# First feed-forward block of a Macaron layer: x kept whole in SBUF, ACT takes half of the norm and the weight copies, column sums in parts, semaphores cleared by ranges

## The reference

```python
x = x + 0.5 * ffn(layernorm(x), router_w, w1, w2)
x = x + mamba(layernorm(x), ...)
x = x + 0.5 * ffn(layernorm(x), router_w, w1, w2)

def ffn(x, router_w, w1, w2):        # 8 experts, hidden 512, top 2
    logits = x @ router_w.T
    top_vals, top_idx = top_k(logits, 2); top_w = softmax(top_vals)
    y[e] = relu(x @ w1[e])**2 @ w2[e]
    return sum over the two chosen experts of top_w * y[expert]
```

## Time and profile before

| what | us |
|---|---|
| three runs | 1326.93, 1328.05, 1328.78 |
| profiled execution | 1326.81, its span 1325.1 |
| first FFN, front | 4 to 71.4 |
| first FFN, sort and pieces | 71.4 to 85.1 and to 109.4 |
| first FFN, experts, to the last scatter | 117.7 to 373 |
| Mamba | 381.4 to 951 |
| second FFN, sort and pieces | 957 to 972.8 and to 997.1 |
| second FFN, experts and end | 1005 to 1258 and to 1325.1 |
| busy over the span | TensorE 1055.2, VectorE 822.2, ACT 607.5, POOL 686.4 |

### The profile page before, as it was taken

How to read it: one execution, slowest core, us unless ns; L and a number is a source line. 1 busy time by engine, 2 the same in 40 slices (tenths; PEclk the granted TensorE clock), 3 DMA queues, 4 the chain that set the end, 5 groups by cost and what they waited for, 6 DMA issues and landing times. The chain is left out here.

```text
span 1325.1 us, 21803 instructions
## 1 busy us (share of the span) xinstructions
PE 1055.2 (80%) x6372; PEld 879.8 (66%) x6404; DVE 822.2 (62%) x1609; ACT 607.5 (46%) x1462; POOL 686.4 (52%) x611
## 2 busy tenths in 40 slices
PE   3747999999915788998889898989447999999900
PEld 3735999999914566666667666666336999999800
DVE  6974444444427899898989897875283444444433
ACT  2312555555513565655656555555213555555400
POOL 6945555555421365655564655567344555555300
PEclk9999999999966898888989898989757999999955
DMA  7761222222232111111111100000152222222187
GB/s 238 254 270 45 76 76 78 77 79 77 57 109 72 48 36 41 41 41 40 41 41 40 40 25 17 17 21 24 49 230 60 77 76 79 77 78 77 53 273 238
DMA packets 73243, 112.20 MB, mean 85 GB/s; under 512 B 10664, under 2 KB 60336, under 8 KB 71856
## 3 DMA queue, kind: packets, MB, share of 16 engines
q1 hardware_dynamic: 47888, 58.77, 13.0%
q0 software_dynamic: 13824, 37.77, 8.8%
q10 hardware_dynamic: 11424, 14.30, 3.2%
HBM read 66.76 MB, written 44.04 MB: 84 GB/s over the span
## 5 line engine op out<-in xcount | busy, mean ns | idle before, releaser
L401 POOL DMA_INDIRECT ys_d<-xs,row_of x144 | 142.0, 986 | 194.4 <-DVE xs L765 188.6
L754 DVE TENSOR_TENSOR xl<-pT,xh 128x256 fp32r<-128x256 f32 x144 | 61.1, 424 | 223.3 <-ACT xh L472 223.3
L459 ACT ACTIVATE hs<-pH 128x512 f32<-128x512 f32 x144 | 86.0, 597 | 233.1 <-PE pH L570 233.1
L396 POOL DMA_INDIRECT xs<-xn_d,token_of x144 | 139.8, 971 | 52.1 <-issue 42.3
L759 DVE TENSOR_TENSOR h2l<-hs,h2h 128x512 fp32r<-128x512 f32 x144 | 99.8, 693 | 77.7 <-ACT h2h L467 77.7
L1534 DVE SCALAR_TENSOR_TENSOR acc<-raw,cwh,acc 128x512 f32<-128x512 f32 x104 | 124.8, 1246 | 2.2 <-POOL acc L1061 1.2
L1157 ACT ACTIVATE ex<-bank,dts 128x128 f32<-128x128 f32 x256 | 72.4, 366 | 98.7 <-PE bank L1302 97.0
L590 PE MATMUL pY<-w2h,h2h 128*128 x576 | 102.9, 300 | 0.4 <-DVE h2l L759 0.3
L570 PE MATMUL pH<-w1h,xh 128*128 x288 | 92.7, 404 | 1.8 <-DVE xl L754 1.0
L570 PE MATMUL pH<-w1l,xh 128*128 x288 | 92.4, 403 | 0.0
L590 PE MATMUL pY<-w2h,h2l 128*128 x576 | 92.2, 282 | 0.0
(11 more groups left out here) (244 smaller groups left out, 2650.1 us busy)
## 6 DMA issues: line engine op xcount, KB each, us to landing
m_yg<-ys_d SPq DMA_DIRECT2D x64, 128.0 KB, 2.1
xs<-ys_d SPq DMA_DIRECT2D x16, 512.0 KB, 5.9
wst<-in_L_ffn_w_dram ACTq DMA_DIRECT2D x8, 512.0 KB, 4.4
xs<-in_L_attn_x_dram SPq DMA_DIRECT2D x8, 512.0 KB, 6.5
hs<-in_L_ffn_w_dram ACTq DMA_DIRECT2D x8, 512.0 KB, 4.8
xn_d<-xs SPq DMA_DIRECT2D x8, 512.0 KB, 3.2
lo_d<-w1l SPq DMA_DIRECT2D x1, 4096.0 KB, 11.1
lo_d<-w2l SPq DMA_DIRECT2D x1, 4096.0 KB, 21.3
```

The source lines that it names most:

```text
L396: pool.indirect_dma_start(out=xg[:, t % NX, :], out_offset=None, in_=xn_d, in_offset=bass.IndirectOffsetOnAxis(ap=token_of[:, t:t + 1], ax ...
L401: pool.indirect_dma_start(out=ys_d, out_offset=bass.IndirectOffsetOnAxis(ap=row_of[:, t:t + 1], axis=0), in_=y[:, t % NX, :], in_offset=No ...
L459: act.activation(r[:, u, :], pH[u][:, :], ACT.Relu).then_inc(relu_done.sem, 1)
```

## The change

In the first FFN, x no longer goes through four places of xs: the low half of w2 (w2l, 128 x 8192) is free until w2's own low parts are made, and all 32 tiles lie there at once (eight loads, at the head of SP's list). VectorE normalises tiles 0 and 1 of each group, ACT tiles 2 and 3 (it needs -mean x rstd for it, `nmr`, one more small VectorE instruction). The weights are loaded by SP's queue, in the order w1 of all experts, then w2 of all experts. ACT makes the high copies: three in the last three groups of the front, five behind the last logits, one after each piece. POOL's sixteen subtractions stand behind its eight pows; those of w2 also wait until xn is stored and turned. The spill is in two: w1l after the load of matrix 11, w2l at the end.

In both FFNs, ohhi_c is made by ACT, as ohhi times one number for each four columns; the rest of the column number, 0 to 3, is added bit by bit with plain ohhi as the weights: the odd ones into the same accumulator, the second bit into pH[0], which VectorE doubles and adds. The iota of column numbers goes.

`Sems.clear` clears ranges of adjacent semaphores in one instruction. FFN1 has 60 semaphores afterwards.

```diff
@@ Sems.clear
-                for s in self.all:
-                    sp.sem_clear(s)
+                nums = sorted(s.num for s in self.all)
+                while nums:
+                    n = 1
+                    while n < len(nums) and nums[n] == nums[0] + n:
+                        n += 1
+                    sp.sem_clear(range(nums[0], nums[0] + n))
+                    nums = nums[n:]
@@ ffn_block, buffers and helpers
-        xa = xs[:, 0:NA * AG, :]
+        xa = w2l[:, :].bitcast(F32).rearrange("p (n d) -> p n d", d=D)
+        NB4 = T // AG
...
-            return (w1 if n % 2 == 0 else w2)[n // 2].rearrange("(k p) n -> p k n", p=P)
+            return (w1 if n < E else w2)[n % E].rearrange("(k p) n -> p k n", p=P)
...
@@ sync
+            def load_weights(n):
+                if n >= NRAW:
+                    sp.wait_ge(w_lo.sem, w_lo.done(n - NRAW))
+                sp.dma_start(wraw(n).rearrange("p (k n) -> p k n", k=KD if n < E else KH), wsrc(n)).then_inc(w_loaded[n % NRAW], 16)
...
-                for h in range(NA):
-                    load(0, h, False)
-                store(0, 0)
-                with sp.Fori(0, rounds - 1) as j:
...
+                for h in range(NB4):
+                    sp.dma_start(xa[:, h * AG:(h + 1) * AG, :], tiles(x, h * (AG * P))).then_inc(xa_loaded[h], 16)
+                for n in range(NRAW):
+                    load_weights(n)
+                for h in range(NB4):
+                    sp.wait_ge(norm_v, (h + 1) * (AG // 2))
+                    sp.wait_ge(norm_a, (h + 1) * (AG // 2))
+                    sp.dma_start(tiles(xn_d, h * (AG * P)), xa[:, h * AG:(h + 1) * AG, :]).then_inc(xn_stored, 16)
+                for n in range(NRAW, NW):
+                    load_weights(n)
+                    if n == E + NRAW - 1:
+                        sp.dma_start(lo_d[0], w1l[:, :].bitcast(F32)).then_inc(w_spilt, 16)
                 sp.wait_ge(w_lo.sem, w_lo.done(NW - 1))
-                sp.dma_start(lo_d[0], w1l[:, :].bitcast(F32)).then_inc(w_spilt, 16)
                 sp.dma_start(lo_d[1], w2l[:, :].bitcast(F32)).then_inc(w_spilt, 16)
@@ gpsimd
-            pool.iota(colnum[:, :], pattern=[[1, C]], base=1, channel_multiplier=0,
-                      allow_small_or_imprecise_dtypes=True)
...
-                for s in range(T // AG + 1):
-                    if s < T // AG:
-                        pows(s // 2, s % 2)
-                    for n in step_weights(s - 1):
-                        lo_weights(n)
-            oh_col.open(pool)
-            for piece in range(C // PC):
-                at, u = slice(piece * PC, (piece + 1) * PC), piece % 2
-                pool.wait_ge(oh_hi.sem, oh_hi.done(piece))
-                pool.tensor_tensor(ohhi_c[:, u, :, :], ohhi[:, u, :, :], along(colnum[:, at], NT), ALU.mult).then_inc(oh_col.sem, 1)
+                for h in range(NB4):
+                    pool.wait_ge(var_done, h + 1)
+                    pool.tensor_tensor(rstd[:, h, :], ve[:, h, :], c["neghalf"][:, 0:AG], ALU.pow).then_inc(pow_done, 1)
+                for n in range(NW):
+                    if n == E:
+                        pool.wait_ge(xn_stored, NB4 * 16)
+                        pool.wait_ge(xT_ready.sem, xT_ready.done(T - 1))
+                    pool.wait_ge(w_hi.sem, w_hi.done(n))
+                    pool.tensor_tensor(wlo(n), wraw(n), whi(n).bitcast(F32), ALU.subtract).then_inc(w_lo.sem, 1)
@@ scalar
+            def hi_weights(n):
+                act.wait_ge(w_loaded[n % NRAW], 16 * (n // NRAW + 1))
+                act.activation(whi(n), wraw(n), ACT.Copy).then_inc(w_hi.sem, 1)
+
+            def normalise(h):
+                act.wait_ge(nmr_done, h + 1)
+                for n in range(AG // 2, AG):
+                    a = xa[:, h * AG + n, :]
+                    act.activation(a, a, ACT.Identity, bias=nmr[:, h, n:n + 1], scale=rstd[:, h, n:n + 1]).then_inc(norm_a, 1)
...
+                normalise(0)
+                for h in range(NB4):
+                    copy_xT(2 * h, 0)
+                    if h > 0:
+                        copy_logits(2 * h - 1)
+                    if h + 1 < NB4:
+                        normalise(h + 1)
+                    copy_xT(2 * h + 1, 1)
+                    copy_logits(2 * h)
+                    if h >= NB4 - 3:
+                        hi_weights(h - (NB4 - 3))
+                copy_logits(T // 2 - 1)
+                for n in range(3, E):
+                    hi_weights(n)
...
                 act.wait_ge(oh_hi.sem, oh_hi.done(piece))
+                if piece >= 2:
+                    act.wait_ge(oh_used.sem, oh_used.done(piece - 2))
                 act.activation(ohhi_p[:, u, :, :], ohhi[:, u, :, :], ACT.Copy, scale=c["part"][:, 0:1]).then_inc(oh_part.sem, 1)
+                for q in range(PC // SUB):
+                    part = slice(q * SUB, (q + 1) * SUB)
+                    last = act.activation(ohhi_c[:, u, part, :], ohhi[:, u, part, :], ACT.Copy, scale=float(piece * PC + q * SUB + 1))
+                last.then_inc(oh_col.sem, 1)
+                if first:
+                    hi_weights(E + piece)
...
+            if first:
+                act.wait_ge(w_lo.sem, w_lo.done(NW - 1))
             relu(0, 0)
@@ tensor, pieces
-                    pe.matmul(pT[0][0:NT, 0:P], ohhi_p[:, piece % 2, n, :], ohlo[:, piece % 2, n, :], **ends)
-                    last = pe.matmul(pT[1][0:NT, 0:P], ohhi_c[:, piece % 2, n, :], ohlo[:, piece % 2, n, :], **ends)
+                    pe.matmul(pT[0][0:NT, 0:P], ohhi_p[:, piece % 2, n, :], lo, start=begin, stop=end)
+                    if n % SUB % 2:
+                        pe.matmul(pT[1][0:NT, 0:P], ohhi[:, piece % 2, n, :], lo, start=False, stop=False)
+                    if n % SUB >= 2:
+                        pe.matmul(pH[0][0:NT, 0:P], ohhi[:, piece % 2, n, :], lo, start=(piece == 0 and n == 2), stop=end)
+                    last = pe.matmul(pT[1][0:NT, 0:P], ohhi_c[:, piece % 2, n, :], lo, start=begin, stop=end)
@@ vector
-                    dve.tensor_scalar(a, a, mv[:, v * AG + n, 0:1], rstd[:, v, n:n + 1], ALU.subtract, ALU.mult).then_inc(norm_done.sem, 1)
-            def hi_weights(n):
-                dve.wait_ge(w_loaded[n % NRAW], 16 * (n // NRAW + 1))
-                dve.tensor_copy(whi(n), wraw(n)).then_inc(w_hi.sem, 1)
...
+                dve.scalar_tensor_tensor(nmr[:, h, :], mv[:, h, :, 0], -1.0, rstd[:, h, :], ALU.mult, ALU.mult).then_inc(nmr_done, 1)
+                for n in range(AG // 2):
...
-            link(dve.tensor_copy(inv2[0:NT, :], pT[1][0:NT, 0:P]))
+            link(dve.tensor_copy(inv[0:NT, :], pT[1][0:NT, 0:P]))
+            link(dve.scalar_tensor_tensor(inv2[0:NT, :], pH[0][0:NT, 0:P], 2.0, inv[0:NT, :], ALU.mult, ALU.add))
```

More of the change, by code:

```diff
@@ L29 @@
 PC = 8
+SUB = 4
 CREDIT = 2
@@ L297, in _ @@
                 sp.dma_start(rw[:, :], router_w).then_inc(rw_loaded, 16)
[L298 to L308, removed]
-                sp.wait_ge(norm_done.sem, norm_done.done((NA * j + h) * AG + (AG - 1)))
-                sp.dma_start(tiles(xn_d, (NA * j + h) * (AG * P)), xa[:, h * AG:(h + 1) * AG, :]).then_inc(xn_stored[h].sem, 16)
+            def load_weights(n):
+                if n >= NRAW:
+                    sp.wait_ge(w_lo.sem, w_lo.done(n - NRAW))
+                sp.dma_start(wraw(n).rearrange("p (k n) -> p k n", k=KD if n < E else KH), wsrc(n)).then_inc(w_loaded[n % NRAW], 16)
             def load_lo(m):
@@ new lines, in turn @@
+                def turn(i):
+                    n = i % AG
+                    if n < AG // 2:
+                        pe.wait_ge(norm_v, i // AG * (AG // 2) + n + 1)
+                    else:
+                        pe.wait_ge(norm_a, i // AG * (AG // 2) + n - AG // 2 + 1)
+                    pe.wait_ge(xT_copied.sem, xT_copied.done(i - 4))
+                    for k in range(KD):
+                        last = pe.transpose(turned[i % 4][:, k * P:(k + 1) * P], xa[:, i, k * P:(k + 1) * P], ident[:, :])
+                    last.then_inc(xT_ready.sem, 1)
@@ new lines, in score @@
+                def score(i):
+                    pe.wait_ge(xT_copied.sem, xT_copied.done(i))
+                    pe.wait_ge(logit_copied.sem, logit_copied.done(i - 2))
+                    for k in range(KD):
+                        last = pe.matmul(pY[i % 2][:, 0:E], xT[:, i % 4, k, :], rwT[:, k, :], start=(k == 0), stop=(k == KD - 1))
+                    last.then_inc(logit_ready.sem, 1)
+                turn(0)
+                turn(1)
+                for i in range(0, T, 2):
+                    if i + 2 < T:
+                        turn(i + 2)
+                        turn(i + 3)
+                    score(i)
+                    score(i + 1)
@@ L599, in _ @@
             turn_x(1)
+            if first:
+                pe.wait_ge(w_lo.sem, w_lo.done(NW - 1))
             pe.wait_ge(experts_known, 1)
@@ L640, in normalise @@
-            def normalise(j, h):
-                v = h % 2
```

(12 more changed lines are left out.)

115 lines of the change are left out of this document (23 added, 92 removed).

## The result

The changed kernel takes **1318.5 us** (median of four executions, 1314.9 to 1325.1) beside 1328.0 us of the kernel before (1326.9 to 1328.8): a ratio of 0.9939, 95% interval 0.9913 to 0.9966, so 9.5 us faster; forecast 1322, by the same step from 1328. The one that was profiled is its slowest, 1325.1 us with a span of 1323.4. Both stand here by stage, in us, measured from start to start of the instructions named. Stretches that the change does not touch are left out: Mamba's memset to its first m_nmr (18.4, 18.3, 18.4), the second FFN's sort (13.6 in all three), its way from the gather to the experts (5.7, 5.5, 5.7) and its final additions (59.0, 60.3, 59.5). The first FFN's last scatter of the kernel before starts at 370.6 us, not at 373.

The account below looks back on a forecast made before the run. Expert stages, full of TensorE, stay untouched; room lay in the first FFN's front (POOL's share largest), both piece loops and block pauses. +7.8 + 1.0 - 4.6 - 0.15 - 9.9 = -5.9 us from 1328.05 gave 1322 us, range 1308 to 1334.

Parts of the forecast that it names:

- Front: First FFN up to the sort: TensorE sets the end, 56.0 us instead of 71.4, a gain of 15.4.
- The front rival: First FFN before the sort: TensorE's clock rises to 2.4 GHz, sort starts at 49 us, total 1316 us; chance 0.18.
- Sort: First FFN's sort: POOL's subtractions exclude VectorE's two-input instructions, +12.3 us, 26.0 us in all, pieces begin at 82.0 us.
- the rival of subtractions that leave VectorE alone: First FFN's sort and pieces: not slowed by POOL, gather at 97 us, total 1299 us; chance 0.10.
- the upper bound of 14.1 us: First FFN's sort: most that POOL's subtractions could add, 6 x 2.35 us, each excluding VectorE for its whole length.
- Pieces with weights: First FFN's piece loop: POOL's subtraction and VectorE exclude each other, 4.2 us a piece, 37.5 us to the gather against 26.7.
- The serial chain of 5.7 us a piece: First FFN's pieces: next ohhi waits for the same piece's subtraction, 5.7 instead of 4.2 us, total 1334 us; chance 0.16.
- The three together: First FFN's front, sort and pieces: first gather starts at 119.5 us instead of 111.7, +7.8 us.
- The spill: First FFN's first gathers: w2's low halves (4 MB) spilled beside them cost +1.0 us, between 0 and 3.
- Second FFN's pieces: Second FFN's piece loop: TensorE's clock rises after two pieces, 19.7 us instead of 24.3, -4.6 us (bounds -0.8 and -4.6).
- The rival that it stays low: Second FFN's pieces: TensorE's clock stays low, with clears at 46 ns, total 1327 us, no change; chance 0.13.
- Clears: Block boundaries: single semaphore clears that go save 50 ns each, -9.9 us (bounds -9.1 and -13).

Follow-up runs that it names:

- e6: Changed kernel with w1's hi copies one a group from the second group on, their loads between the stores of xn: 1316.5 us.
- e7: Changed kernel with POOL's subtractions from the fourth on held until the first ohhi is made, after the sort: 1322.7 us.
- e4: Changed kernel with both spills of the low halves held until 8 and 16 tiles are scattered: 1314.8 us, ratio 0.9891.
- e9: Changed kernel with pads, so that every tile has its address of the kernel before, new small tiles last: 1315.5 us, ratio 0.9914.
- e5: Kernel before with the range clears and the new column sums together, without the new front: 1305.3 us, ratio 0.9835.
- e1_again: Changed kernel run and profiled once more with no edit: 1317.7 us, ratio 0.9930.
- e8: Changed kernel with late spills, gate instructions behind the row numbers and weight halves made all over the front: 1303.7 us, ratio 0.9819.
- e10: Changed kernel with the edits of e8 and e9 together: 1300.1 us, ratio 0.9798.
- e2: Kernel before with the range clears alone: 1318.4 us, ratio 0.9928.
- e3: Kernel before with the new column sums alone (ohhi_c on ScalarE, 24 matmuls a piece), in both FFNs: 1318.1 us, ratio 0.9931.

## Why the prediction was right, and where its terms were off

The direction and the time held, 1318.5 us against 1322, inside the range, and so did the mechanisms of the front, the sort, the pieces and the clears. The price of the spill did not, and the sum is near in part by luck. Step by step:

- *Front.* The mechanism was right: TensorE full at its low pace. The start was mis-sized by 1.9 us: the first x landed at 8.1 us, nearer still to the bound of 7.9 than the 8.7 taken, and the first transposes came 4.4 us behind it instead of 5.8: the chain taken from the kernel before held a wait of VectorE of 1.13 us for the second group of x (13.50 us in its timeline), which is not there with the new order of the loads. The remaining 1.6 us are in the tiles and the end term: 39.9 us from the first transposes to the sort, where 32 tiles at 1.25 us and 1.5 us behind them make 41.5. Sort at 52.4 us instead of 56.0. The front rival (clock rises) did not happen.
- *Sort.* +10.2 us for a forecast of +12.3. The exclusion was the right mechanism (e6 and e7 move the sort with POOL's time beside it); the rival of subtractions that leave VectorE alone, 1299 us, is out. Of the upper bound of 14.1 us POOL had 13.84 us under the sort, but VectorE slips one instruction in at each seam between two subtractions, six in all, which the step did not count; and an instruction with one input (L671) was held, which the step had excluded.
- *Pieces with weights.* 34.8 us for 37.5. From the first ohhi to the eighth it is 25.6 us, 3.65 a piece where the step took 4.2 (3.8 us less in all), and from there to the gather 9.2 instead of 8.1. The serial chain of 5.7 us a piece, the rival on the slow side, did not come. What the end has over its term shows in the trace: VectorE's gate instructions, queued ahead of the copy of the sums, were themselves held, 2.33 and 1.88 us beside POOL's last two subtractions, so that the copy starts at 108.49 us, 1.0 us after the last matmul's end at 107.53:

```profile
103.59 2.33 DVE L720 TENSOR_SCALAR top<-top 128x32 f32<-128x32 f32 x1
105.95 0.35 DVE L721 RECIPROCAL top<-top 128x32 f32<-128x32 f32 x1
106.34 1.88 DVE L722 TENSOR_SCALAR gates<-top 128x32 f32<-128x32 f32 x1
...
108.49 0.29 DVE L725 COPY inv<-pT 72x128 f32<-72x128 f32 x1
```

- *The three together* put the gather at 111.0 us, 0.7 us earlier than before, where +7.8 was forecast: an error of 8.5 us, made of 3.6 in the front, 2.2 in the sort and 2.7 in the pieces.
- *The spill.* This is the step that failed: "+1.0, between 0 and 3 us". It is +6.3 us (e4). The bound came from one transfer of 512 KB in front of a gather; this one has 4 MB, takes 13.2 us, and the rows of a gather behind it come when it has landed. That the sum came near the truth is luck: 8.5 us at the gather and 2.4 in the clears one way stand against 5.3 here and 2.5 in the expert stages the other way.
- *Second FFN's pieces.* -4.6 us for -4.6: the clock rose after two pieces, as forecast (matmuls 0.107, then 0.056 us apart), granted 0.83 over the stage instead of 0.50, and from the first ohhi to the last matmul it is 19.4 us for 19.7. The rival that it stays low is out.
- *Clears.* -12.3 us for -9.9. Of the 5.8 us of idle time at Mamba's end 5.0 were clears: 62 ns each over the three places, near the upper end of 67 ns, where the step took 50 from the difference of two boundaries.
- *Not in the forecast.* +1.4 and +1.1 us in the expert stages (the tile addresses, e9, give 0.02 us a tile, 1.4 us over 72), and Mamba's length, which moves by up to 8 us from one execution to another.

The parts taken alone say more than the sum. Clears and column sums are worth 22 us together (e5). The new order of x and weights, which gives TensorE 19 us in the front, returns them in the sort, the pieces, the spill and the addresses, and costs 12 to 13 us on top of e5. Between the spans of e5 and e1_again, 12.4 us, 10.0 lie ahead of the experts (113.4 and 123.4 us), 2.3 in the two expert stages and 1.1 in the last additions, while Mamba was 1.4 us shorter in e1_again. The new order becomes worth having only when the weight halves are really made under the front and the spill is late: e8's experts start 7.1 us ahead of e5's, though its median is only 1.6 us lower (Mamba 553.3 us in its profile against 547.3), less than the spread of its runs; e10, with the old addresses, is 5.2 us under e5.

## What to carry to other kernels

Before work of POOL is moved, find a stretch in which VectorE is idle; beside a busy VectorE a subtraction of 2.36 us costs about three quarters of its length (10.2 of 13.84 us of them in the sort, 3.0 of 4.04 in e6). A large transfer that nobody waits for goes behind the first gathers of a stage that runs ahead of its data, not in front of them. And measure each part of a change alone on the old kernel: a gain of 9 us hid two parts worth 22 and one that cost 13.

## What the runs showed of the hardware

- Mamba's length varies though no edit changes its instructions: 544.6 to 546.0 us in three profiles (e1, e2, e9), 547.3 to 547.4 in four (before, e3, e5, e10), 549.9 in one (e7) and 552.4 to 553.7 in four (after, e4, e6, e8). The four of 547.4 us have the same granted clock in the same eighths of the stage: 0.74, 0.91, 0.87, 0.94, 0.90, 0.88, 0.93, 0.90. In the others it differs: e2 has 0.73, 0.90, 0.88, 0.88, 0.95, 0.95, 0.90, 0.90, and of the long ones after has 0.67, 0.87, 0.87, 0.91 in the first half and then the values of the four. All long ones are kernels with the new front at the new addresses, but one kernel can be short and long (e1_again and after), so what chooses stays open. The executions of the kernel before differ as well, by 8 us on one chip (1325.2 to 1333.2) and by 10 us on another (1323.2 to 1333.5); the four beside the result, within 2 us, were too few to show it. For the changed kernel, 7.7 of the 8.8 us between the two profiles are Mamba.
- A single semaphore clear costs 62 ns of a block boundary (65, 60 and 63 ns at the three places). What a clear over a range costs was not measured apart.
- TensorE's down matmuls of a tile take 0.02 us more or less with the addresses of the tiles in SBUF, 1.4 us over 72 tiles, at the same granted clock (1.00 in the middle of both stages).
